# Expert stage of an attention + routed feed-forward kernel: blocks one by one, or in pairs

## The reference, cut to what matters

```
x = x + attention(layernorm(x), ctx)            # 32 x 256 x 512, 16 heads
n = layernorm(x)
scores = einsum('sp,tp->st', pe, sign(tile_sigs))
idx = argmax(scores, axis=-1)                   # one expert of 8 for each position
y_all = einsum('bsd,tod->bsto', n, W) + b
out = x + take(y_all, idx)
```

## Time and profile before

| | |
|---|---|
| median of 3 runs | 964.98 us (964.84 to 965.28) |
| the profiled execution's own time | 966.44 us |
| its span, first to last instruction | 964.5 us |
| granted TensorE clock, mean | 0.979 |
| PE busy | 908.4 us (94%) |
| DVE busy | 734.6 us (76%) |
| POOL busy | 571.2 us (59%) |
| ACT busy | 384.0 us (40%) |

### The profile page before, as it was taken

The page is one execution under the profiler, slowest core; times in us unless marked ns, Lnnn a source line. Parts: engine busy times, 40 slices in busy tenths (PEclk is TensorE's granted clock), DMA queues, the critical chain, the costliest instruction groups (busy, mean ns, idle before and its releaser), DMA issues.

```text
span 964.5 us, 16646 instructions
## 1 busy us (share of the span) xinstructions
PE 908.4 (94%) x5696; PEld 729.2 (76%) x5697; DVE 734.6 (76%) x1097; ACT 384.0 (40%) x697; POOL 571.2 (59%) x764
## 2 busy tenths in 40 slices
PE   5889999999999999999999999999718999999997
PEld 3668878878878878878878878887516888888885
DVE  5788777687787678788677787779766777777775
ACT  5355444444544445444444545444532111111110
POOL 4346557464654745556464655744675777777773
PEclk9899999999999999999999999999977999999999
DMA  9423131331313223131331313114624445545551
GB/s 339 155 108 112 55 101 56 111 100 55 112 45 113 65 90 112 56 100 56 111 91 60 116 45 112 56 45 134 227 83 126 151 163 163 163 156 162 164 164 48
DMA packets 48876, 108.10 MB, mean 112 GB/s; under 512 B 10496, under 2 KB 15136, under 8 KB 46624
## 3 DMA queue, kind: packets, MB, share of 16 engines
q1 hardware_dynamic: 36928, 71.39, 23.2%
q0 software_dynamic: 11200, 35.21, 11.4%
q10 hardware_dynamic: 672, 0.52, 0.2%
HBM read 73.47 MB, written 35.19 MB: 113 GB/s over the span
## 4 chain that ended last, share of the span: by engine, by line
PE 90%; POOL 2%; DVE 2%; DMA 2%; ACT 1%; issue 1%; SPq 1%; DVEq 0%; ACTq 0%; POOLq 0%
PE pS L1356 28%; PE pA L1645 21%; PE pA L1356 19%; PE pS L1414 7%; PE pA L1437 7%; PE pT L1425 5%; PE pT L1625 3%; DMA xt_raw<-in_x_t 1%; PE pS L1382 1%; DMA wf_hl<-in_wf 1%; POOL xt_lo L980 1%; POOL wf_hl L303 0%; POOL y L996 0%; SPq L913 0%; DVE row L1204 0%
## 5 line engine op out<-in xcount | busy, mean ns | idle before, releaser
L1645 PE MATMUL pA<-wf_hl,x_hi 128*128 x560 | 183.0, 408 | 0.0
L1199 DVE TENSOR_TENSOR s<-pS,bias 128x1024 f32<-128x1024 f32 x64 | 78.2, 1222 | 106.8 <-PE pS L1414 105.2
L996 POOL COPY y<-y_mom 128x1 f32<-128x1 f32 x64 | 16.1, 251 | 238.8 <-DVE y_mom L1238 238.8
L1013 POOL TENSOR_TENSOR s<-s,row 128x1024 f32<-128x1024 f32 x64 | 121.9, 1905 | 16.3 <-DVE row L1219 16.3
L1543 POOL DMA_INDIRECT out_dram<-y,scatter_rows x70 | 94.8, 1355 | 54.3 <-DVE y L1591 54.3
L1115 ACT CAST ot_hi<-pA 128x512 fp32r<-128x512 f32 x64 | 37.6, 588 | 224.2 <-PE pA L1437 224.2
L1645 PEld LDWEIGHTS pA<-wf_hl,x_hi 128*128 128x128 f32 x560 | 100.9, 190 | 19.2 <-issue 0.3
L1562 ACT CAST x_hi<-pT 128x512 fp32r<-128x512 f32 x70 | 41.1, 587 | 186.1 <-PE pT L1625 152.6
L1356 PE MATMUL pA<-wo_hi,ot_hi 128*128 128x512 f32 x256 | 108.8, 425 | 4.5 <-DVE ot_lo L1223 4.5
L1645 PE MATMUL pA<-wf_hl,x_lo 128*128 x280 | 111.2, 397 | 0.0
L980 POOL TENSOR_TENSOR xt_lo<-xt_raw,xt_hi 128x512 fp32r<-128x512 f32 x64 | 95.1, 1520 | 21.1 <-ACT xt_hi L1071 21.1
(11 more groups left out here) (124 smaller groups left out, 1907.3 us busy)
## 6 DMA issues: line engine op xcount, KB each, us to landing
x_scratch<-y SPq DMA_DIRECT2D x64, 257.0 KB, 3.0
xt_raw<-in_x_t SPq DMA_DIRECT2D x16, 1024.0 KB, 6.1
x<-in_x SPq DMA_DIRECT2D x64, 256.0 KB, 2.6
wf_hl<-in_wf SPq DMA_DIRECT2D x8, 1024.0 KB, 8.8
ctx_raw<-in_ctx_t SPq DMA_DIRECT2D x32, 128.0 KB, 3.1
bias_all<-in_bf SPq DMA_DIRECT2D x1, 2048.0 KB, 9.7
mask_early<-in_mask SPq DMA_DIRECT2D x1, 1536.0 KB, 13.6
xg<-x_scratch,gather_rows POOLq DMA_INDIRECT x70, 3.5
```

Of the source, the lines that this page charges most:

```text
L1013: pool.tensor_tensor(p, p, h.row[:, t % h.c, 3, :].unsqueeze(2).broadcast_to([P, H, BK]), ALU.mult)\
L1199: dve.tensor_tensor(h.s_sb[:, t % h.c, :].rearrange("p (h k) -> p h k", h=H), pS[:, 0, :].rearrange("p (h k) -> p h k", h=H), h.bias[:, t ...
L1645: mm = pe.matmul(pA[:, r % 2, :], a[:, c * P:(c + 1) * P], w, start=(c == 0 and m == 0), stop=(c == KC - 1 and m == 2))
```

## The change

`xb`, `xn2`, `x2_hi` and `x2_lo` get four buffers in place of two, and the waits that guard them reach back three blocks in place of one. PE takes the blocks in pairs: the transposes of blocks i+2 and i+3 (eight instructions), then the products of blocks i and i+1, with all 70 blocks written out in place of the loop. The expert's number is now read right ahead of each product, no longer ahead of the transposes. DVE's order is rewritten in pairs. PSUM banks, gathered rows (six), `y2` (three), ACT's order and POOL's order stay.

```diff
-        xb = sb("xb", [P, 2, DM])
-        xn2 = sb("xn2", [P, 2, DM])
-        x2_hi = sb("x2_hi", [P, 2, DM], F32R)
-        x2_lo = sb("x2_lo", [P, 2, DM], F32R)
+        xb = sb("xb", [P, 4, DM])
+        xn2 = sb("xn2", [P, 4, DM])
+        x2_hi = sb("x2_hi", [P, 4, DM], F32R)
+        x2_lo = sb("x2_lo", [P, 4, DM], F32R)
...
             def high(j):
                 act.wait_ge(x2t_done, j + 1)
-                wait(act, f_done, j - 1)
+                wait(act, f_done, j - 3)
...
             def add_bias(j):
                 e = dve.value_load(expert_of[0:1, j:j + 1], min_val=0, max_val=NE - 1)
+                wait(dve, y2_ready, j - 3)
...
             def normalise(j):
                 r = j % R
-                wait(dve, x2t_done, j - 1)
+                wait(dve, x2t_done, j - 3)
...
             def low(j):
                 dve.wait_ge(x2_hi_ready, j + 1)
+                wait(dve, f_done, j - 3)
...
             normalise(0)
+            normalise(1)
             low(0)
-            normalise(1)
+            low(1)
+            normalise(2)
+            normalise(3)
             add_bias(0)
-            for j in range(NR):
-                if j + 1 < NR:
-                    low(j + 1)
-                if j + 2 < NR:
-                    normalise(j + 2)
-                if j == 0:
+            for i in range(0, NR, 2):
+                for j in (i + 2, i + 3):
+                    if j < NR:
+                        low(j)
+                if i == 0:
                     expert_low(dve, 3).then_inc(wf_lo_ready, NE - 3)
-                finish(j)
-                if j + 1 < NR:
-                    add_bias(j + 1)
+                add_bias(i + 1)
+                for j in (i + 4, i + 5):
+                    if j < NR:
+                        normalise(j)
+                finish(i)
+                if i + 2 < NR:
+                    add_bias(i + 2)
+                finish(i + 1)
...
-            turns = (NR - 5 - 1) // R
-            for n in range(-1, R):
-                body(0, n)
-            with pe.Fori(1, turns) as k:
-                for n in range(R):
-                    body(k, n)
-            for n in range(NR + 1 - R * turns):
-                body(turns, n)
+            transpose(0)
+            transpose(1)
+            for i in range(0, NR, 2):
+                for j in (i + 2, i + 3):
+                    if j < NR:
+                        transpose(j)
+                product(i, expert(i))
+                product(i + 1, expert(i + 1))
```

More of the change, by code:

```diff
@@ L1560, in high @@
                 act.wait_ge(x2t_done, j + 1)
-                wait(act, f_done, j - 1)
-                act.copy(x2_hi[:, j % 2, :], pT[:, j % 2, :]).then_inc(x2_hi_ready, 1)
+                wait(act, f_done, j - 3)
+                act.copy(x2_hi[:, j % 4, :], pT[:, j % 2, :]).then_inc(x2_hi_ready, 1)
             for j in range(NR):
@@ L1569, in add_bias @@
                 e = dve.value_load(expert_of[0:1, j:j + 1], min_val=0, max_val=NE - 1)
-                dve.tensor_tensor(xb[:, j % 2, :], xg[:, j % R, 0:DM],
+                wait(dve, y2_ready, j - 3)
+                dve.tensor_tensor(xb[:, j % 4, :], xg[:, j % R, 0:DM],
                                   bias_all[:, bass.ds(e, 1), :].rearrange("p a n -> p (a n)"), ALU.add)\
@@ L1575, in normalise @@
                 r = j % R
-                wait(dve, x2t_done, j - 1)
+                wait(dve, x2t_done, j - 3)
                 dve.wait_ge(gathered[r], 16 * (j // R) + 16)
-                dve.tensor_scalar(xn2[:, j % 2, :], xg[:, r, 0:DM], xg[:, r, DM:DM + 1], xg[:, r, DM + 1:DM + 2],
+                dve.tensor_scalar(xn2[:, j % 4, :], xg[:, r, 0:DM], xg[:, r, DM:DM + 1], xg[:, r, DM + 1:DM + 2],
                                   ALU.subtract, ALU.mult).then_inc(xn2_ready, 1)
@@ L1582, in low @@
                 dve.wait_ge(x2_hi_ready, j + 1)
-                dve.tensor_tensor(x2_lo[:, j % 2, :], pT[:, j % 2, :], x2_hi[:, j % 2, :].bitcast(F32), ALU.subtract)\
+                wait(dve, f_done, j - 3)
+                dve.tensor_tensor(x2_lo[:, j % 4, :], pT[:, j % 2, :], x2_hi[:, j % 4, :].bitcast(F32), ALU.subtract)\
                     .then_inc(x2_lo_ready, 1)
@@ L1590, in finish @@
                 dve.wait_ge(xb_ready, j + 1)
-                dve.tensor_tensor(y2[:, j % 3, :], pA[:, j % 2, :], xb[:, j % 2, :], ALU.add).then_inc(y2_ready, 1)
+                dve.tensor_tensor(y2[:, j % 3, :], pA[:, j % 2, :], xb[:, j % 4, :], ALU.add).then_inc(y2_ready, 1)
             dve.wait_ge(bias_loaded, 16)
@@ L1597, in experts_vector, with transpose @@
             normalise(0)
+            normalise(1)
             low(0)
-            normalise(1)
+            low(1)
+            normalise(2)
+            normalise(3)
             add_bias(0)
-            for j in range(NR):
-                if j + 1 < NR:
-                    low(j + 1)
-                if j + 2 < NR:
-                    normalise(j + 2)
-                if j == 0:
-                    expert_low(dve, 3).then_inc(wf_lo_ready, NE - 3)
-                finish(j)
-                if j + 1 < NR:
-                    add_bias(j + 1)
-        def experts_tensor(pe):
[L1613 to L1621, removed]
+            for i in range(0, NR, 2):
[3 more added lines that the diff above has]
+                if i == 0:
+                    expert_low(dve, 3).then_inc(wf_lo_ready, NE - 3)
+                add_bias(i + 1)
[6 more added lines that the diff above has]
+                finish(i + 1)
+        def experts_tensor(pe):
+            def transpose(j):
                 pe.wait_ge(xn2_ready, j + 1)
@@ L1624, in transpose, with expert, product @@
                 for c in range(KC):
-                    mm = pe.transpose(pT[:, r % 2, c * P:(c + 1) * P], xn2[:, r % 2, c * P:(c + 1) * P], ident[:])
+                    mm = pe.transpose(pT[:, j % 2, c * P:(c + 1) * P], xn2[:, j % 4, c * P:(c + 1) * P], ident[:])
                 mm.then_inc(x2t_done, 1)
-            def expert(k, n):
-                j, r, turn = at(k, n)
-                e = pe.value_load(expert_of[0:1, bass.ds(j, 1)], min_val=0, max_val=NE - 1)
+            def expert(j):
+                e = pe.value_load(expert_of[0:1, j:j + 1], min_val=0, max_val=NE - 1)
                 pe.wait_ge(wf_lo_ready, e + 1)
                 return e
-            def product(k, n, e):
-                j, r, turn = at(k, n)
+            def product(j, e):
                 wait(pe, y2_ready, j - 1)
                 pe.wait_ge(x2_lo_ready, j + 1)
-                hi, lo = x2_hi[:, r % 2, :], x2_lo[:, r % 2, :]
+                hi, lo = x2_hi[:, j % 4, :], x2_lo[:, j % 4, :]
                 for c in range(KC):
@@ L1644, in product @@
                         w = wf_hl[:, bass.ds(e, 1), o:o + DM].rearrange("p a n -> p (a n)")
-                        mm = pe.matmul(pA[:, r % 2, :], a[:, c * P:(c + 1) * P], w,
+                        mm = pe.matmul(pA[:, j % 2, :], a[:, c * P:(c + 1) * P], w,
                                        start=(c == 0 and m == 0), stop=(c == KC - 1 and m == 2))
                 mm.then_inc(f_done, 1)
[L1649 to L1658, removed]
-            turns = (NR - 5 - 1) // R
-            for n in range(-1, R):
-                body(0, n)
-            with pe.Fori(1, turns) as k:
-                for n in range(R):
-                    body(k, n)
-            for n in range(NR + 1 - R * turns):
-                body(turns, n)
+            transpose(0)
[6 more added lines that the diff above has]
+                product(i + 1, expert(i + 1))
         with nc.Block() as block:
```

## The result

The changed kernel takes 1048.51 us (median, 1047.17 to 1049.74) against 965.13 us beside it: the ratio is 1.0861, with a 95% interval of 1.0842 to 1.0881. It is 83.4 us slower; 95.1 were forecast. The profiled execution took 1047.41 us at a span of 1045.3 us and a mean clock of 0.964.

A forecast was written before the change was run, and what follows sets the result against it. PE bounds the kernel at 6.48 us a pair; the change closes a DVE-POOL-gather loop of 9.49 us. Over 32 pairs, with start and end, that adds 95.1 us to 964.98: 1060 us, range 1035 to 1083.

The forecast's parts named there:

- The loop: Expert stage: finish(i-2), two scatters and two gathers on POOL, landing, normalise(i+5), finish(i) form a closed chain.
- Its size: Sum of the links from finish(i-2) to finish(i): 9.49 us a pair, against 6.48 on PE.
- The scatter behind finish(i-2): First scatter on POOL in the loop, beside an add_bias on DVE: 1.39 us, the median.
- The second scatter: Scatter(i-1) on POOL in the loop, overlapped by add_bias(i+1) for its first 0.2 us only: 1.20 us.
- landing to normalise: End of the loop: gather(i+5) from start to landing 3.50 us, then 0.10 to normalise(i+5).
- The start: Start of the expert stage: first product from 731.7 to 736.1, finish(0) near 737.0 us.
- The end: After finish(64) at 1040.7: product(66) 0.73 us later, products 66 to 69 unhindered at 2.80 each, to 1052.6.
- rival 2: TensorE falls to its lower clock: hidden if one spell a pair, 1156 us if whole pairs; 6 in 100.
- Eight transposes in a row, and the reads of the number: On PE: eight cost what two times four do; reads before products bounded by 0 and 0.3 us, charged nothing.
- Rival 1: The loop does not close and PE stays the bound at 6.48 us a pair: 966.7 or 965 us; 3 in 100.
- The signs: Profile: normalise waits for gathers some 33 times, finish not for PE, PE idles some 3 us a pair, POOL issues without waits.
- The rule on the shared port: Two-input SBUF VectorE instruction blocks GpSimd's SBUF reads until it ends: second scatter 0.99 + 0.2 us, time 1060.

The follow-up runs named there:

- e1: Changed kernel with eight buffers for gathered rows in place of six: 966.3 us, ratio 1.0016 to the kernel before.
- e2: Changed kernel with POOL issuing gather(j+6) just ahead of scatter(j), six buffers kept: 1007.56 us, ratio 1.0435 to the kernel before.
- e6: Changed kernel with seven buffers for gathered rows in place of six: 968.23 us, ratio 1.0017 to the kernel before.
- e3: Changed kernel with x2_lo by W_hi left out, eight matmuls per expert product, not twelve: 1045.41 us, ratio 1.0818 to the kernel before.
- e9: Kernel before with x2_lo by W_hi left out, eight matmuls per expert product, not twelve: 921.54 us, ratio 0.9544.
- e5: Changed kernel with DVE's order finish(i), add_bias(i+2), normalise(i+5), finish(i+1): 987.65 us, ratio 1.0222 to the kernel before.
- e8: Kernel of e5 with both experts' numbers read on TensorE ahead of the pair's transposes: 974.58 us, ratio 1.0089 to the kernel before.
- e7: Kernel before with last tile's statistics ahead of two expert-weight pieces on POOL, DVE's low halves waiting for them: 958.89 us, ratio 0.9927.
- e4: Changed kernel with normalise(i+5) moved behind finish(i) on DVE: 998.37 us, ratio 1.033 to the kernel before.

## Why the prediction was right, point by point

- **The loop.** It was forecast from the order on DVE and POOL's waits alone, and it is there link by link. e1, e2 and e6 change its members and move the time as its sum says; e3 and e9 show that TensorE has left the path with the change and was on it before.
- **Its size** was the term that missed: 9.49 us forecast, 9.08 measured over the 31 pairs from finish(2) to finish(64). The scatter behind finish(i-2) took 1.21 us and not 1.39. An add_bias lies beside it, but it starts 0.60 us after finish and not 0.85 as in the earlier trace rows, so less of it is left when the scatter begins. The second scatter took 1.01 and not 1.20: add_bias(i+1) ends at 864.53, just ahead of it. The third, landing to normalise, took 3.54 with the landing, against 3.60. Over 32 pairs this is -13.1 us.
- **The start.** Finish(0) came at 733.8 and not 737.0; 2.8 us of that is the first gather, which started at 717.95 and not 720.75 us, ahead of anything that the change touches.
- **The end.** From finish(64) to the end of the last product I had 11.9 us; it was 14.1. The first product after the loop began 1.08 us after finish(64) and not 0.73, with the read of the expert's number bare (0.29 us), and then ran at the low clock: 4.6 us to the finish behind it and not 2.80. The last of the rows on rival 2 below show both. That the start and the end nearly cancel, at -3.2 and +2.1 us, is luck. In sum -3.2 - 13.1 + 2.1 = -14.2 us on 95.1, which is the 80.8 us between the two spans. The medians differ by 83.4, since the profiled execution of before was 1.3 us above the median beside it and that of after 1.1 us below.
- **Eight transposes in a row, and the reads of the number**, were charged nothing. e1 bears this out where the rows come early. e5 and e8 show the condition: where the last transposes' wait ends late, the read is bare and costs about 0.35 us a pair (12 us), within the 0 to 0.3 us a product that I had as bounds. The cover that I named, PE's idle time in the loop, was there in the changed kernel.
- **Rival 1** (the loop does not close) fell with the result; it is what e1 makes of the kernel. **Rival 2** (the lower clock) was half right on the clock and right on the price. The mean clock of the stage is 0.94. A pair with a low spell, and the next one without:

```profile
860.00:869.00 9.00, 7.71 (x28) 6.05 (x29) 4.68 (x8) 0.83 (x2) 4.17 (x4) 0.81 0.34 117
869.00:878.00 9.00, 7.56 (x37) 5.72 (x35) 4.69 (x8) 1.75 (x3) 4.17 (x4) 1.00 0.37 117
```

The first took 869.93 - 860.86 = 9.07 us, the second, to the finish at 879.01, 9.08. All 31 pairs from finish(2) to finish(64) say the same: in ten the clock was 0.81 and PE was busy for 8.27 to 8.51 us, in the other 21 it was 1.00 and PE was busy for 6.95 to 7.17, and the ten took 9.06 us on average, the 21 took 9.09. So the lower clock is hidden inside the loop, with 0.7 us to spare. It shows only at the end, where no loop hides it:

```profile
1024.45 0.66 PE L1626 MATMUL pT<-ident,xn 128*128 128x128 f32 x4 [1.80 <-DVE xn L1579]
1025.40 1.22 PE L1644 MATMUL pA<-wf_hl,x_hi 128*128 x2 [0.29 <-issue]
1026.41 0.63 PE L1644 MATMUL pA<-wf_hl,x_lo 128*128 x1
1026.84 1.06 PE L1644 MATMUL pA<-wf_hl,x_hi 128*128 x2
1027.69 0.63 PE L1644 MATMUL pA<-wf_hl,x_lo 128*128 x1
1028.12 0.94 PE L1644 MATMUL pA<-wf_hl,x_hi 128*128 x2
1028.90 0.39 PE L1644 MATMUL pA<-wf_hl,x_lo 128*128 x1
```

Two matmuls lie 0.43 us apart there, 0.23 after 1028.9.

- **The signs.** The gathers' waits, POOL's order without a gap, and a finish that no longer waits for PE inside the loop all came. Two sizes did not. Normalise waited 65 times and not some 33, since gather(i+4) comes late as well; its wait is not on the loop, which runs through gather(i+5). And PE was to work near 6.5 us a pair and idle for 3: it was busy for 7.0 and idle for 2.1, and in the ten pairs with a low spell busy for 8.4 and idle for 0.7.
- **The rule on the shared port** (the Trainium skill, SBUF — State Buffer, "Who interferes with whom") would have the second scatter at 1.19 us, the median row at 1.39. It took 1.01, since the add_bias ended before it began, and 1.01 again in e9; the first, with 0.32 us of an add_bias left at its start, took 1.21. The trace agrees with the rule where the add_bias is already running when POOL starts: from 740 to 1020 us the 31 such issues took longer by what was left of it less 0.1 us (1.21 with 0.31 to 0.32 left, 1.41 with 0.52). It does not where the add_bias starts second. In the turn shown above, gather(i+4) began at 863.33 and an add_bias at 863.85, beside it for 0.46 us; the gather took 0.98 us and the add_bias its usual 0.68, and all the other 93 issues of that stretch, this kind among them, took 0.97 to 1.01 us. The same section holds, as an inference, that a VectorE instruction of this kind leaves the making of a transfer's descriptors alone; the stretched scatters speak against that.

What was not tried: whether pairs bring anything on an engine queue that is less ahead than here, and what brings the low clock in the loop. The eight transposes alone do not: with the same transposes the clock was 1.00 in e1, without idle time, and in e2 with some (PE busy for 158.91 of 180 us).

## What to carry to other kernels

When instructions are regrouped, count for each buffer how far its release now lies ahead of its next use on the engine that waits in order, and add up every link between them, the queue of a third engine included. Here the busy shares showed room on DVE and POOL, and the lead of the gathers fell from four blocks to none while the number of buffers for them stayed; one more buffer, or one instruction put elsewhere, was worth 50 to 80 us. An order that makes a large loss can still be worth nothing once the loss is mended: look for gain where the critical engine is idle, as at the border of the two stages.

## What the runs showed of the hardware

- An indirect transfer's issue on POOL took 0.97 to 1.01 us in the changed kernel's loop where no DVE instruction with two operands in SBUF was running at its start, even if one began while it ran. Where one was running, the issue took longer by nearly what was left of it: up to 1.5 us beside an add_bias. Beside the long subtractions of e7, which stand in a row, it took 3.07 us. The data of a stretched gather landed later by as much (4.03 us from start to use in e8 and not 3.54).
- Three POOL instructions of one column took 2.24, 2.27 and 2.46 us beside DVE's long subtractions, and 0.19, 0.22 and 0.57 us without them.
- Behind a wait that ends late, the read of a register from memory costs time that is otherwise hidden: 0.49 us ahead of an add_bias on DVE (e4), and about 0.35 us a pair on TensorE (e5 against e8).
